# Cross-attention and quantised feed-forward on one core: context and key weights in three chunks, keys over eight banks, low parts shared out anew

## What is computed

```python
def reference(x, ctx, Wq, Wk, Wv, Wo, bo, clip_x, clip_down, w_gate, w_up, w_down):
    # x (8, 512, 512), ctx (8, 77, 384), 8 heads of 64
    q, k, v = layernorm(x) @ Wq, ctx @ Wk, ctx @ Wv          # split by head
    x = x + softmax(q @ k.T / 8) @ v @ Wo + bo               # merged by head
    xq = act_fake_quant(layernorm(x), clip_x)                # 8 bit, one scale for all
    h = silu(xq @ wq8(w_gate).T) * (xq @ wq8(w_up).T)        # weights 8 bit, a scale per row
    return x + act_fake_quant(h, clip_down) @ wq8(w_down).T
```

## Time and profile before

| | us |
|---|---|
| median of 3 runs | 563.48 |
| lowest and highest run | 563.13 and 565.64 |
| the profiled execution | 564.18 |
| its span, first to last instruction | 562.4 |
| TensorE busy in the span | 533.8 |
| VectorE / ScalarE / GpSimd busy | 471.0 / 293.3 / 234.8 |

### The profile page before, as it was taken

How to read it: one execution, slowest core, us unless ns; L and a number is a source line. 1 busy time by engine, 2 the same in 40 slices (tenths; PEclk the granted TensorE clock), 3 DMA queues, 4 the chain that set the end, 5 groups by cost and what they waited for, 6 DMA issues and landing times.

```text
span 562.4 us, 7992 instructions
## 1 busy us (share of the span) xinstructions
PE 533.8 (95%) x2691; PEld 354.2 (63%) x2699; DVE 471.0 (84%) x874; ACT 293.3 (52%) x408; POOL 234.8 (42%) x352
## 2 busy tenths in 40 slices
PE   4999889999999999999789899999999999899997
PEld 1978668787888878787668644444444446343443
DVE  2747888999989898998987699999989988879883
ACT  3744546556555655544343555555554543999300
POOL 3576748769596876856542000000000000055441
PEclk9999999999999999999999999999999999999999
DMA  8717465765667574536294928750343130399987
GB/s 307 262 41 265 120 201 156 229 211 173 201 224 240 183 238 145 168 98 197 62 295 174 286 45 297 268 160 13 103 113 74 39 76 2 114 339 217 114 110 117
DMA packets 82338, 93.82 MB, mean 167 GB/s; under 512 B 46609, under 2 KB 49425, under 8 KB 82041
## 3 DMA queue, kind: packets, MB, share of 16 engines
q1 hardware_dynamic: 77973, 85.44, 47.9%
q0 software_dynamic: 4320, 7.87, 9.6%
q10 hardware_dynamic: 4, 0.00, 0.0%
HBM read 47.51 MB, written 37.78 MB: 152 GB/s over the span
## 4 chain that ended last, share of the span: by engine, by line
PE 46%; issue 34%; DVE 13%; DMA 5%; ACT 1%; POOL 1%; SPq 0%; POOLq 0%; DVEq 0%
PE QO L194 6%; PE QO L196 5%; PE QO L195 5%; PE SP L382 4%; PE WOP L495 3%; PE WOP L493 3%; PE WOP L494 3%; DMA out<-n2b 2%; PE PTP L1088 2%; PE QO L1088 2%; PE SP L1088 2%; PE PTP L430 2%; DVE P L401 1%; DVE mx L394 1%; DVE x L519 1%
## 5 line engine op out<-in xcount | busy, mean ns | idle before, releaser
L45 POOL DMA_DIRECT2D out<-n2b x30 | 30.2, 1039 | 213.8 <-DVE n2b L1099 213.8
L989 ACT ACTIVATE sil<-QO,fsc 128x512 f32<-128x512 f32 x88 | 60.5, 687 | 72.9 <-PE QO L983 72.9
L983 PE MATMUL QO<-nT,wgu 128*128 128x512 bf16 x352 | 90.4, 379 | 1.0 <-ACT nT L221 0.6
L983 PE MATMUL SP<-nT,wgu 128*128 128x512 bf16 x352 | 90.3, 379 | 0.0
L993 DVE SCALAR_TENSOR_TENSOR h<-SP,fsc,sil 128x512 f32<-128x512 f32 x88 | 65.9, 749 | 10.6 <-PE SP L983 10.4
L422 POOL TENSOR_TENSOR PN<-P,rs 128x512 f32<-128x512 f32 x64 | 44.3, 713 | 57.1 <-DVE rs L414 57.1
L996 DVE TENSOR_REDUCE hmx<-h 128x1 f32<-128x512 f32 x88 | 60.4, 686 | 3.0
L405 ACT ACTIVATE P<-P,r 128x616 f32<-128x616 f32 x32 | 25.9, 811 | 69.7 <-DVE P L401 69.7
L983 PEld LDWEIGHTS QO<-nT,wgu 128*128 128x128 bf16 x352 | 34.3, 98 | 42.7 <-DMA nT<-qb 1.1
L983 PEld LDWEIGHTS SP<-nT,wgu 128*128 128x128 bf16 x352 | 34.4, 98 | 41.5
L194 PE MATMUL QO<-xTs,wqs 128*128 128x512 f32 x128 | 52.0, 406 | 2.9 <-DVE xTs L225 2.6
(11 more groups left out here) (169 smaller groups left out, 1125.9 us busy)
## 6 DMA issues: line engine op xcount, KB each, us to landing
xTr<-in_xT SPq DMA_DIRECT2D x8, 1024.0 KB, 7.6
xn<-in_x SPq DMA_DIRECT2D x32, 256.0 KB, 3.8
out<-x SPq DMA_DIRECT2D x32, 256.0 KB, 2.9
n_rows<-n SPq DMA_DIRECT2D x32, 256.0 KB, 2.6
n2b<-n_rows SPq DMA_DIRECT2D x32, 256.0 KB, 3.9
out<-n2b POOLq DMA_DIRECT2D x30, 256.0 KB, 4.5
h_spill<-h SPq DMA_DIRECT2D x2, 2816.0 KB, 9.4
h<-h_spill SPq DMA_DIRECT2D x6, 768.0 KB, 8.0
```

What stands on the lines that cost most here:

```text
L983: m = e.matmul(ps, wv_[:, k, col:col + 128], nT[:, b % 2, :, k, :], start=(k == 0), stop=(k == 3))
L989: t_sil[n] = add("act", lambda e: e.activation(sil[:, n % SR, :], gp, ACT.Silu, scale=fsc[:, ic:ic + 1]), [t_g[n], t_fs, t_h.get(n - SR)] ...
```

## The change

Context and Wk are loaded chunk by chunk, context on SP's queue and Wk on ACT's, in the order chunk 0, chunk 1, Wq (half on each queue), chunk 2. The two `clips` loads go to SP behind the bias. Each chunk is split as it comes, context and Wk in turn. The key matmuls run chunk by chunk over all eight PSUM banks: chunk 0 by part (high x high for seven products, then each of the others), chunk 1, chunk 2; the eighth product, in WOP, comes last. VectorE adds up the four chunks of Wq and a single matmul with ones makes the column sum, in the middle of chunk 1. Wq's low parts: chunks 0 and 1 on GpSimd, 2 and 3 on VectorE; those of the first x tile: 0, 1 and 2 on VectorE, 3 on GpSimd. The first query product waits chunk by chunk. Wo's high part stands behind the first copy out of a query bank.

```diff
-        state = {"use": 0, "banks": [QO[:, 0:512], QO[:, 512:1024], PTP[:, 0:512], PTP[:, 512:1024]],
-                 "free": [()] * 4}
+        state = {"use": 0, "banks": [QO[:, 0:512], QO[:, 512:1024]], "free": [(), ()]}
...
-        t_wq = dma("sp", wqr[:, :, :], Wq.rearrange("(k p) n -> p k n", p=128), [], "ld_wq")
-        t_ctx = dma("sp", ctr[:, :, :], ctxT.rearrange("(k p) n -> p k n", p=128), [], "ld_ctx")
-        t_wk = dma("sp", wkr[:, :, :], Wk.rearrange("(k p) n -> p k n", p=128), [], "ld_wk")
...
+        def load_k(k):
+            dma("sp", ctr[:, k, :], ctx_v[k], [], f"ld_k{k}")
+            t_lk[k] = dma("act", wkr[:, k, :], wk_v[k], [], f"ld_k{k}")
+
+        load_k(0)
+        load_k(1)
+        dma("sp", wqr[:, 0:2, :], wq_v[:, 0:2, :], [], "ld_wq")
+        t_wq = dma("act", wqr[:, 2:4, :], wq_v[:, 2:4, :], [], "ld_wq")
+        load_k(2)
...
-        dma("act", clips[0:1, 0:1], clip_x.rearrange("(a n) -> a n", a=1), [], "ld_clip")
-        t_clip = dma("act", clips[0:1, 1:2], clip_h.rearrange("(a n) -> a n", a=1), [], "ld_clip")
+        dma("sp", clips[0:1, 0:1], clip_x.rearrange("(a n) -> a n", a=1), [], "ld_clip")
+        t_clip = dma("sp", clips[0:1, 1:2], clip_h.rearrange("(a n) -> a n", a=1), [], "ld_clip")
...
-        t_cs = add("pe", colsum, [t_ones, t_wq], "wq_sum")
...
+        def split_k(k):
+            t_ch[k] = copy("act", cts[:, 0, k, :], ctr[:, k, :], [t_lk[k]], "sp_hi")
+            t_kh[k] = copy("act", wks[:, 0, k, :], wkr[:, k, :], [t_lk[k]], "sp_hi")
+            t_cl[k] = less("dve", cts[:, 1, k, :], ctr[:, k, :], cts[:, 0, k, :], [t_ch[k]], "sp_lo")
+            t_kw[k] = less("dve", wks[:, 1, k, :], wkr[:, k, :], wks[:, 0, k, :], [t_kh[k]], "sp_lo")
+
+        k_banks = [QO[:, 0:512], QO[:, 512:1024], SP[:, 0:512], SP[:, 512:1024], PTP[:, 0:512],
+                   PTP[:, 512:1024], MI[:, :], WOP[:, :]]
...
+            def fn(e):
+                for i in which:
+                    r = e.matmul(k_banks[m][:, 0:308], wks[:, int(i == 1), k, w], cts[:, int(i == 2), k, s],
+                                 start=(k == 0 and i == 0), stop=(k == 2 and i == 1))
+                return r
...
+        split_k(0)
+        split_k(1)
+        wsum = [vst[:, 0, i, :].bitcast(f32) for i in range(2)]
+        t_s0 = add("dve", lambda e: e.tensor_tensor(wsum[0], wqr[:, 0, :], wqr[:, 1, :], ALU.add), [t_wq],
+                   "sp_lo")
+        t_s1 = add("dve", lambda e: e.tensor_tensor(wsum[1], wqr[:, 2, :], wqr[:, 3, :], ALU.add), [t_wq],
+                   "sp_lo")
+        t_s1 = add("dve", lambda e: e.tensor_tensor(wsum[0], wsum[0], wsum[1], ALU.add), [t_s0, t_s1], "sp_lo")
+        for i, waits in ((0, [t_ch[0], t_kh[0]]), (2, [t_cl[0]]), (1, [t_kw[0]])):
+            for m in range(7):
+                k_mm(m, 0, (i,), waits)
+        for m in range(7):
+            k_mm(m, 1, (0, 2, 1), [t_ch[1], t_kh[1], t_cl[1], t_kw[1]])
+            if m == 3:
+                t_cs = add("pe", lambda e: e.matmul(WOP[:, :], ones[:, :], wsum[0], start=True, stop=True),
+                           [t_ones, t_s1], "wq_sum")
...
+        def split_wq(k, engine):
+            t = copy("act", wqs[:, 0, k, :], wqr[:, k, :], [t_wqc[k]], "sp_hi")
+            t_wql[k] = less(engine, wqs[:, 1, k, :], wqr[:, k, :], wqs[:, 0, k, :], [t], "wq_lo_" + engine)
+
+        def first_xT(k, engine):
+            t = copy("act", xTs[:, 0, k, :], xTr[:, k, :], [t_xT[0]], "xT_hi")
+            t_xl[k] = less(engine, xTs[:, 1, k, :], xTr[:, k, :], xTs[:, 0, k, :], [t], "xT_lo_" + engine)
...
+        split_k(2)
+        for k in range(4):
+            centre(k)
+        t_ctxl, t_wkl = t_cl[2], t_kw[2]
+        t_km = {m: k_mm(m, 2, (0, 2, 1), [t_ctxl, t_wkl]) for m in range(7)}
+        for k in range(3):
+            t_km[7] = k_mm(7, k, (0, 2, 1), [t_wqc[3]])
+        split_wq(0, "pool")
+        split_wq(1, "pool")
+        first_xT(0, "dve")
+        k_out(0)
+        first_xT(1, "dve")
+        split_wq(2, "dve")
+        split_wq(3, "dve")
+        first_xT(2, "dve")
+        first_xT(3, "pool")
+        for m in range(1, 8):
+            k_out(m)
...
+            if (b, m) == (0, 0):
+                at, bank = 0, state["banks"][0]
+                state["use"] = 1
+                for k in range(4):
+                    def fn(e, k=k):
+                        e.matmul(bank, pairs[k][0], pairs[k][2], start=(k == 0), stop=False)
+                        e.matmul(bank, pairs[k][0], pairs[k][3], start=False, stop=False)
+                        return e.matmul(bank, pairs[k][1], pairs[k][2], start=False, stop=(k == 3))
+                    t_qh[b, m] = add("pe", fn, [*state["free"][0], t_wql[k], t_xl[k]], "qo_mm")
...
-        t_woh = copy("act", wos[:, 0], wor[:, :, :], [t_wo], "wo_hi")
         t_wol = None
         for m in range(4):
             q_chunk(0, m)
+            if m == 0:
+                t_woh = copy("act", wos[:, 0], wor[:, :, :], [t_wo], "wo_hi")
```

More of the change, by code:

```diff
@@ L263, in block_kernel @@
         t_idF, t_idB = t_id
-        def colsum(e):
-            for k in range(4):
-                m = e.matmul(WOP[:, :], ones[:, :], wqr[:, k, :], start=(k == 0), stop=(k == 3))
-            return m
-        t_cs = add("pe", colsum, [t_ones, t_wq], "wq_sum")
-        for k in range(3):
-            t = copy("act", cts[:, 0, k, :], ctr[:, k, :], [t_ctx], "sp_hi")
-            t_ctxl = less("dve", cts[:, 1, k, :], ctr[:, k, :], cts[:, 0, k, :], [t], "sp_lo")
-        for k in range(3):
-            t = copy("act", wks[:, 0, k, :], wkr[:, k, :], [t_wk], "sp_hi")
-            t_wkl = less("dve", wks[:, 1, k, :], wkr[:, k, :], wks[:, 0, k, :], [t], "sp_lo")
@@ L281, in k_part @@
-        def k_part(half, j):
+        t_ch, t_cl, t_kh, t_kw = {}, {}, {}, {}
+        def split_k(k):
[5 more added lines that the diff above has]
+                   PTP[:, 512:1024], MI[:, :], WOP[:, :]]
@@ L282, in k_part, with k_mm @@
+        def k_mm(m, k, which, waits):
+            half, j = m // 4, m % 4
             s = slice(half * 308, half * 308 + 308)
             w = slice(j * 128, j * 128 + 128)
-            b4 = slice(4 * half, 4 * half + 4)
-            pairs = [(wks[:, 0, k, w], wks[:, 1, k, w], cts[:, 0, k, s], cts[:, 1, k, s])
-                     for k in range(3)]
-            at, bank, t = qo_bank(pairs, 308, 128, [t_ctxl, t_wkl])
-            state["free"][at] = tuple(
-                copy(engine, kst[64 * g:64 * g + 64, b4, j, L * g:L * g + L],
-                     bank[64 * g:64 * g + 64, :].rearrange("p (b l) -> p b l", b=4), [t, t_kz], "K_" + engine)
-                for g, engine in enumerate(("act", "dve")))
@@ new lines, in k_mm @@
+            return add("pe", fn, waits, "qo_mm")
+        split_k(0)
[6 more added lines that the diff above has]
+        t_s1 = add("dve", lambda e: e.tensor_tensor(wsum[0], wsum[0], wsum[1], ALU.add), [t_s0, t_s1], "sp_lo")
@@ new lines, in block_kernel, with centre @@
+        for i, waits in ((0, [t_ch[0], t_kh[0]]), (2, [t_cl[0]]), (1, [t_kw[0]])):
[6 more added lines that the diff above has]
+                           [t_ones, t_s1], "wq_sum")
+        t_wqc, t_xl, t_wql = {}, {}, {}
+        def centre(k):
+            t_wqc[k] = add("dve", lambda e: e.scalar_tensor_tensor(
+                out=wqr[:, k, :], in0=WOP[:, :], scalar=-1.0 / D, in1=wqr[:, k, :],
+                op0=ALU.mult, op1=ALU.add), [t_cs], "wq_c")
@@ new lines, in split_wq, with k_out @@
+        def split_wq(k, engine):
[4 more added lines that the diff above has]
+            t_xl[k] = less(engine, xTs[:, 1, k, :], xTr[:, k, :], xTs[:, 0, k, :], [t], "xT_lo_" + engine)
+        t_kl = {}
+        def k_out(m):
+            half, j = m // 4, m % 4
+            b4 = slice(4 * half, 4 * half + 4)
+            for g, engine in enumerate(("act", "dve")):
+                t_kl[m, g] = copy(engine, kst[64 * g:64 * g + 64, b4, j, L * g:L * g + L],
+                                  k_banks[m][64 * g:64 * g + 64, 0:308].rearrange("p (b l) -> p b l", b=4),
+                                  [t_km[m], t_kz], "K_" + engine)
@@ L315, in block_kernel @@
+        for m in range(1, 8):
+            k_out(m)
+        t_k01 = [(t_kl[m, 0], t_kl[m, 1]) for m in range(2)]
+        t_kl = [t_kl[7, 0], t_kl[7, 1]]
+        t_xTs = {0: [t_xl[2], t_xl[3]]}
+        t_xT[1] = load_xT(1, t_xTs[0])
         t_c = ("wq_c", 4)
-        state["banks"] = state["banks"][0:2]
+        state["free"][0:2] = t_k01
         t_v = Tokens()
@@ L352, in q_chunk @@
                      for k in range(4)]
[L353 removed]
+            if (b, m) == (0, 0):
[7 more added lines that the diff above has]
+                    t_qh[b, m] = add("pe", fn, [*state["free"][0], t_wql[k], t_xl[k]], "qo_mm")
+            else:
+                at, bank, t_qh[b, m] = qo_bank(pairs, 512, 128, [t_wql[1], t_wql[3], *t_xTs[b]])
             t_q[b] = copy("act", qs[:, b % 2, m, :], bank,
[L355 removed]
```

(1 more changed line is left out.)

26 lines of the change are left out of this document (4 added, 22 removed).

## The result

The changed kernel takes 560.75 us (median of 11 runs, 559.08 to 562.93); the kernel before, run beside it, 563.44 us. The ratio is 0.9946, with an interval of 0.9933 to 0.9960: some 3 us faster. Run once more beside other kernels it gave 0.9938 [0.9917, 0.9958]. The forecast was 562.6 in a range of 560.0 to 564.2: the direction and the range held, but the gain is three times the 0.9 us that the sum gave, and it lies at the very bound of 0.5% that the prediction counted as no change.

A forecast was written before the change was run, and what follows sets the result against it. TensorE, busy 95% of the span, was taken as the bound, with a serial start-up. A 3.87 us earlier first query, less waits of 1.75 and 1.25, left about 0.9: 563.48 to 562.6 us, range 560.0 to 564.2.

The forecast's parts named there:

- the column sum: Amid the key matmuls: one matmul costs 0.88 us on TensorE's path; VectorE's additions, ending near 11.5, hide behind slow key matmuls.
- the sum: Whole kernel: 3.87 us gained at the first query, less 1.75 and 1.25 of waits, gives 0.87, say 0.9 us.
- The start: Start-up: chunk 0 at 5.1 to 5.2, first key matmul 6.45, first query matmul 20.04 against 23.91, 3.87 us earlier.
- slow pace: First key matmuls: TensorE at half rate until about 11.35, losing 2.45 us; the least certain term.
- The turns: First query steps: VectorE and GpSimd low parts wait for each other's whole instruction; third query step 1.75 us late, value rows 32.75.
- The next meeting: Second x tile: VectorE's low parts wait for GpSimd's low part of Wo until 36.5, taking 1.25 us; 0.85 us gain remains.
- waits of at most 1.1 us: VectorE beside GpSimd's low part of Wo: if each wait is this short, the gain is 2.0 us instead of 0.85.
- No turns: Rival: the waits for the first x tile's and Wo's low parts do not occur; all 3.8 us stay, 559.7; 14%.
- No earlier start: Rival, start-up loads: queued transfers mix into chunk 0, landing at 6.4 or later; start slips 1.3 us, 563.5 to 564; 11%.
- A TensorE that stays slow: Rival, key matmuls: waits between groups keep TensorE at half rate; slow through all keys, 4.8 us later, 568; 6%.

The follow-up runs named there:

- the matmuls of ones: Changed kernel plus twelve small f32 matmuls of ones with ones on TensorE ahead of the key matmuls, result unused: 560.03 us, 0.9936.
- the run of three edits: Changed kernel plus twelve matmuls of ones ahead of the keys, Wo's low part ahead of the row statistics, one first low part alone on GpSimd: 557.36 us, 0.9892.
- the fills: Changed kernel with GpSimd's three low parts of the first x tile and Wq each replaced by three memsets that read nothing: 557.93 us, 0.9905.
- the old sharing: Changed kernel with low parts shared as before: all four of Wq and x's 1 and 3 on GpSimd, x's 0 and 2 on VectorE: 561.68 us, 0.9973.
- on one queue: Changed kernel with all start-up loads on SP's queue, in the same order: 559.76 us, 0.9939.
- the three kernels that also moved Wo's low part: Changed kernel with three edits (ones, Wo first, one GpSimd low part), 557.36 us; plus early feed-forward loads and one queue, 557.90; those five without ones, 557.53.

## Why the prediction was right, and where its sizes were not

**The start** came as worked out: chunk 0 taken up at 5.05 (5.1 to 5.2), first key matmul 6.43 (6.45), slow pace until 11.42 (11.35). The twenty slow matmuls cost 2.28 us (5.13 for 20, against 20 x 0.1425; the sum had 2.45), the column sum 0.84 (0.88): first query at 19.76 (20.04). The run with the matmuls of ones shows that the slow pace lies on the path, with 1.4 us of it left once the column sum loses its cover. That the two queues share one rate was not quite right: on two queues chunk 0 is 0.6 us later than on one, and chunk 1 earlier.

**The turns** are shown, by the run in which GpSimd only writes. The term was 1.75 and measured 1.40 (from 21.13, when six query matmuls were done, to 22.53). Its start was mis-sized by the same plan: the first low part began at 16.98, not 17.35, and the last ended at 22.38 instead of 23.05. So of the 0.62 by which the value rows beat 32.75, 0.28 is the start's and 0.35 the wait's.

**The next meeting** is the term that was most wrong in size. The prediction had Wo's low part 1.4 us later than before, at 31.9, and took 1.25 for it. It started at 30.74, 0.21 later. The chain was right (low parts, key copies, Wv, row statistics, then GpSimd), but the seven key copies were priced at 0.5 each, the duration of one alone in the earlier trace rows. Back to back they start 0.39 apart (0.88 for two): 2.85 us for the row of them, not 3.5. With the 0.67 above, Wv's low part ended 1.2 earlier than I had it. The pair on VectorE did wait for Wo's low part as described, took 3.00 us, and ended at 36.48 instead of 37.75. Of the 2.71 us at the value rows 0.62 were lost there, so 2.09 remain where the sum had 0.87. The run with Wo's low part first confirms the mechanism. The 2.09 is close to the 2.0 that the prediction gave for waits of at most 1.1 us, but by chance: the first of the pair took 2.40 instead of 0.69, a wait of 1.7 us.

That the wait lasts through the whole long instruction was left open between two values. The Trainium skill (SBUF — State Buffer, Who interferes with whom) says that a VectorE instruction with two SBUF inputs contends with a GpSimd instruction that reads SBUF, not with one that only writes it, and that the shared ports are an exclusive lock. The trace agrees with both, by the 6.32 us beside 4.80 in the run of three edits and by the 0.69 beside the fills. So the longer of the two values was the right one, and the size failed elsewhere.

**Behind it** the prediction took the gain to stay as it was. It grew by 0.6 to 0.8 at the third x tile, since VectorE there meets GpSimd at another point of the same turns (0.84 us into its pair, 0.20 before), and by 0.3 near 216 us. Those 0.9 to 1.1 us are the other part of what was missed; 2.09 and 0.9 make the 2.99 of the trace and the 2.7 to 3.2 of the medians. The rest of the profiled pair's difference (4.5 of the span) accrues behind 290 us, in places that the change doesn't touch, and isn't in the medians.

**The rivals.** No turns: shown wrong for the changed kernel; the run that took the first of them away is 2.8 us faster by the medians, 1.6 by the trace at 290 us. No earlier start: wrong. A TensorE that stays slow did not occur at the keys, but its kind did elsewhere, with the old sharing, with one low part on GpSimd and with the ones.

**The size.** The range held, but the time lies only 0.75 us above its lower bound, at three times the gain of the sum. The three terms all erred the same way (0.28, 0.35 and 0.63), and the growth behind came on top.

**What stays open:** why the feed-forward load came at 57.91 in one execution with the ones and at 55.04 in one with the three edits. About half of that is its issue (48.19 and 46.78); why it then took 9.7 us in one and 8.3 in the other is not shown. With the fills it came at 56.00, on one queue at 56.78, so it was not tied to 57.9.

## What to carry to other kernels

When a chain of waits is shortened at its head, follow the operands of the next stage through the engine that makes them, at the pitch that its instructions have back to back, before taking a gain or a loss from it; the size of a gain hung here on seven copies at 0.39 instead of 0.5. Two engines that both read the same memory should be given work so that a long instruction of one falls into a stretch where the other has nothing of that kind, and a wait that is taken away can come back at the next meeting: giving GpSimd one low part alone brought nothing by itself (561.42 us), while the three kernels that also moved Wo's low part, with other edits beside, took 557.4 to 557.9. It need not come back: with the fills the second score product kept all of the gain. The long instruction that is moved must not fall on the next operand either: in the run of three edits Wo's low part, moved forward, made Wv's last one take 5.11 us and cost the value rows 0.3. A wait of TensorE may cost more than its length, so compare the pace of the matmuls behind it.
